# A rewritten order of VectorE's and GpSimd's work in the second attention slot of a fused graph-network kernel

## The reference

```
h = relu(layernorm(x))
# layer 0: each node takes the maximum over the features of its first 25 neighbours
idx, valid = top_k of (-column number) where adj != 0, 25 of them
agg = max over the valid neighbours of h ; max with 0 if the node has 25 neighbours or fewer
x = x + relu(concat[h, agg] @ W + b)
h = relu(layernorm(x))
# layer 1: attention of 8 heads of 16, open where adj, its transpose or the diagonal is set,
# then a feed-forward of 512 and two layernorms with scales and shifts
q, k, v = split(h @ Wqkv.T + bqkv)
attn = softmax(where(adj | adj.T | eye, q k / 4, -inf)) @ v
y = layernorm(h + attn @ Wo.T + bo) ; y = layernorm(y + relu(y @ W1.T + b1) @ W2.T + b2)
x = x + y
```

## Time and profile before

| what | value |
|---|---|
| median of 3 runs | 1257.94 us (1255.73 to 1259.4) |
| the profiled execution | 1255.8 us, span 1253.8 us |
| mean granted TensorE clock | 0.943 |
| TensorE matmul busy | 1043.9 us, 83% |
| VectorE busy | 797.5 us, 64% |
| ScalarE busy | 805.7 us, 64% |
| GpSimd busy | 737.4 us, 59% |

### The profile page before, as it was taken

How to read it: one execution, slowest core, us unless ns; L and a number is a source line. 1 busy time by engine, 2 the same in 40 slices (tenths; PEclk the granted TensorE clock), 3 DMA queues, 4 the chain that set the end, 5 groups by cost and what they waited for, 6 DMA issues and landing times.

```text
span 1253.8 us, 29308 instructions
## 1 busy us (share of the span) xinstructions
PE 1043.9 (83%) x11014; PEld 405.0 (32%) x11014; DVE 797.5 (64%) x3053; ACT 805.7 (64%) x1031; POOL 737.4 (59%) x741
## 2 busy tenths in 40 slices
PE   0125587688984989999999999999999999999874
PEld 0112331233331334343434333433343334333222
DVE  7856877767788477977797769776363534122323
ACT  1321257677852867788778877887678756875541
POOL 4776677567777777777777777776777520000000
PEclk9567889899996999999999999999999999999996
DMA  6533336426423433453345334431242110000000
GB/s 188 167 67 107 104 94 160 145 70 140 119 67 113 110 111 106 123 105 104 110 127 105 100 114 126 104 93 52 80 70 71 53 52 18 21 1 10 10 9 8
DMA packets 95156, 110.77 MB, mean 88 GB/s; under 512 B 17080, under 2 KB 75968, under 8 KB 94976
## 3 DMA queue, kind: packets, MB, share of 16 engines
q1 hardware_dynamic: 68352, 62.67, 16.4%
q0 software_dynamic: 22816, 44.61, 15.5%
q10 hardware_dynamic: 3808, 1.19, 0.4%
HBM read 91.10 MB, written 12.85 MB: 83 GB/s over the span
## 4 chain that ended last, share of the span: by engine, by line
PE 64%; ACT 11%; DVE 7%; POOL 7%; issue 6%; DMA 3%; SPq 0%; DVEq 0%; POOLq 0%; ACTq 0%
PE sc L1664 20%; PE cb L1684 13%; ACT probs L1460 10%; PE sc L1668 7%; PE m L1741 5%; PE m L1749 5%; POOL nb_low L716 3%; PE m L1570 3%; POOL nb_low L694 2%; PE m L1593 2%; DMA nb_low<-h_rows,lsorted 1%; PE m L1723 1%; PE m L1598 1%; PE m L1792 1%; PE m L1771 1%
## 5 line engine op out<-in xcount | busy, mean ns | idle before, releaser
L1460 ACT ACTIVATE probs<-sc 128x1024 f32<-128x1024 f32 x512 | 496.7, 1023 | 245.8 <-PE sc L1668 242.4
L694 POOL DMA_INDIRECT nb_low<-h_rows,lsorted x474 | 470.3, 992 | 168.8 <-issue 129.1
L1684 PE MATMUL cb<-probs,va 128*17 128x512 f32 x2048 | 270.6, 600 | 4.1 <-issue 3.2
L1664 PE MATMUL sc<-q_near,k_g 32*128 32x512 f32 x1024 | 147.8, 647 | 21.4 <-ACT probs L1460 17.2
L1664 PE MATMUL sc<-q_far,k_g 32*128 32x512 f32 x1024 | 149.6, 654 | 16.9 <-ACT probs L1460 15.8
L1015 DVE TENSOR_REDUCE agg<-nb_low 128x128 f32<-128x1024 f32 (+10 forms) x58 | 96.3, 1660 | 60.2 <-DMA nb_low<-h_rows,lsorted 34.4
L1668 PE MATMUL sc<-barred,negident 32*32 32x512 bf16 x4096 | 112.5, 386 | 1.8 <-issue 1.8
L829 DVE MAX8 cand<-keys 128x8 f16<-128x128 f16 x512 | 105.3, 278 | 2.2
L716 POOL DMA_INDIRECT nb_low<-h_rows,first_lists x80 | 80.5, 1006 | 41.9 <-issue 22.5
L1668 PEld LDWEIGHTS sc<-barred,negident 32*32 32x32 bf16 x4096 | 35.4, 88 | 200.8 <-issue 200.8
L1452 ACT ACTIVATE barred<-m 128x512 bf16<-128x512 f32 x128 | 72.9, 608 | 39.5 <-PE m L1598 39.5
(11 more groups left out here) (180 smaller groups left out, 1442.2 us busy)
## 6 DMA issues: line engine op xcount, KB each, us to landing
adj_t<-in_adj_dram SPq DMA_DIRECT2D x64, 512.0 KB
nb_low<-h_rows,lsorted POOLq DMA_INDIRECT x474
xh<-in_x_dram SPq DMA_DIRECT2D x8, 512.0 KB
h_rows<-xh SPq DMA_DIRECT2D x8, 512.0 KB
hl<-h_rows SPq DMA_DIRECT2D x8, 512.0 KB
x<-in_x_dram SPq DMA_DIRECT2D x16, 256.0 KB
out_dram<-h2T SPq DMA_DIRECT2D x16, 256.0 KB, 3.2
ag<-pooled_rows SPq DMA_DIRECT2D x7, 512.0 KB
```

The lines of the kernel that those rows point to most:

```text
L694: pool.indirect_dma_start(out=dst, out_offset=None, in_=h_rows[0:(f + 1) * (N + 1), :], in_offset=bass.IndirectOffsetOnAxis(ap=lsorted[:, ...
L1460: nc.scalar.activation(probs[:, i % 2, 2 * pair:2 * pair + 2, :], sc[:, 2 * pair:2 * pair + 2, :], ACT.Exp, scale=SCALE).then_inc(s_probs, 1)
L1664: nc.tensor.matmul(sc[:, a, :], k[part, :], q[part, :], start=True, stop=False)
L1684: last = nc.tensor.matmul(cb[a * SPAN:a * SPAN + VW, :], va[:, u % 2, a, kt, :], probs[:, i % 2, a, :], start=(kt == 0), stop=(kt == T - 1))
```

## The change

1. VectorE's slot 1: `second_slot` has a new order and its end is written out as `second_slot_end`. Ahead of the linear part of graph 2 now stand only `list_tile(4, 0)`, `list_tile(4, 1)` and `merge_pair(0)`; tiles 2, 3 and 4 of graph 4 and `merge_pair(2)` come behind it. `context(1, 2)` stands ahead of graph 3's first pooled tiles. `add_input(0, 1)` comes before `pool_tile(2, 6)`, `first_norm(4)` behind `context(1, 1)`.
2. In slot 2, `context(1, 3)` comes ahead of `pool_tile(3, 3)`.
3. GpSimd gathers tile 7 of graph 2 before it scatters graph 3's lists; `send(2, 6)` follows the scatter, then `load_lists(3)`, `send(2, 7)` and `beta2(1)`. The paces of graph 2's tiles 5 to 7 and of graph 3's tiles 0 to 2 are earlier by up to three steps.
4. SyncE: graph 1's `turn_values` goes ahead of adjacency tile (3, 5) in slot 0; in slot 1 the tiles (4, 4) and (4, 5) go behind the x1 halves, and `turn_values(2, 0)` ahead of tile (4, 7).
5. Graph 2's rank steps are 21 and 22 in place of 19 and 21; ScalarE normalizes graph 3's x at steps 24 and 25 of slot 0 in place of 22 and 23 (`H_AT_3`).

```diff
-PACE_2 = [(25, 3, 0, 31), (32, 3, 1, 35), (35, 3, 1, 38), (38, 3, 1, 41), (41, 3, 1, 43), (43, 3, 1, 45), (45, 3, 2, 47), (49, 3, 0, 50)]
-PACE_3 = [(19, 4, 0, 24), (24, 4, 0, 26), (27, 4, 0, 29), (29, 3, 0, 31), (32, 3, 0, 34), (35, 3, 1, 37), (38, 3, 0, 39), (43, 3, 2, 45)]
+PACE_2 = [(25, 3, 0, 31), (32, 3, 1, 35), (35, 3, 1, 38), (38, 3, 1, 41), (41, 3, 1, 43), (42, 3, 0, 44), (44, 3, 0, 46), (46, 3, 0, 48)]
+PACE_3 = [(18, 4, 0, 23), (23, 3, 0, 26), (26, 3, 0, 29), (29, 3, 0, 31), (32, 3, 0, 34), (35, 3, 1, 37), (38, 3, 0, 39), (43, 3, 2, 45)]
...
+H_AT_3 = {24: (0, 4), 25: (4, 8)}
...
-RANK_AT = {0: (-2, 3, 7, 8), 1: (0, 0, 2, 4), 2: (0, 19, 21, None), 3: (1, 11, 12, None)}
+RANK_AT = {0: (-2, 3, 7, 8), 1: (0, 0, 2, 4), 2: (0, 21, 22, None), 3: (1, 11, 12, None)}
...
-                    for t in range(2, 6):
+                    for t in range(2, 5):
                         load_list_tile(3, t)
                     turn_values(1, 0)
+                    load_list_tile(3, 5)
...
-                        for t in range(2, 5):
+                        for t in range(2, 4 if s == 1 else 5):
                             load_list_tile(l, t)
...
+                    if s == 1:
+                        load_list_tile(4, 4)
+                        load_list_tile(4, 5)
                     if live(l):
                         load_list_tile(l, 6)
                         store_h_rows(l)
+                    if s == 1:
+                        turn_values(f, 0)
+                    if live(l):
                         load_list_tile(l, 7)
-                    if live(g) and live(f):
+                    if live(g) and live(f) and s > 1:
                         turn_values(f, 0)
...
-                        if t == T - 2 and f >= AHEAD:
+                        if t == T - 2 and f > AHEAD:
...
+                    if f == AHEAD:
+                        scatter_lists(f + 1)
+                        send(f, T - 2)
...
                             load_lists(f + 1)
+                        if f > AHEAD:
+                            send(f, T - 2)
                         if f >= AHEAD:
-                            send(f, T - 2)
                             send(f, T - 1)
+                        if f == AHEAD:
+                            beta2(f - 1)
...
+                    context(1, 0)
                     pool_tile(2, 3)
-                    context(1, 0)
                     crowded_tiles(3)
                     make_lists(3)
                     pool_tile(2, 4)
                     list_ranks(3)
+                    add_input(0, 0)
+                    pool_tile(2, 5)
                     list_tile(4, 0)
-                    add_input(0, 0)
-                    first_norm(4)
                     finish(0, 0)
-                    pool_tile(2, 5)
-                    list_tile(4, 1)
-                    merge_pair(0)
                     wide_maxima(1, 1)
+                    add_input(0, 1)
                     pool_tile(2, 6)
-                    add_input(0, 1)
-                    list_tile(4, 2)
+                    pool_tile(2, 7)
                     finish(0, 1)
                     context(1, 1)
-                    pool_tile(2, 7)
+                    list_tile(4, 1)
+                    first_norm(4)
+                    merge_pair(0)
+
+                def second_slot_end():
+                    linear(2)
+                    list_tile(4, 2)
                     list_tile(4, 3)
+                    context(1, 2)
+                    largest(2, 0)
                     merge_pair(2)
+                    largest(2, 1)
+                    low_levels(3)
+                    largest(2, 2)
+                    pool_tile(3, 0)
+                    largest(2, 3)
+                    products(2)
+                    flag(2)
+                    list_tile(4, 4)
+                    pool_tile(3, 1)
+                    list_tile(4, 5)
+                    merge_pair(4)
+                    pool_tile(3, 2)
+                    list_tile(4, 6)
+                    list_tile(4, 7)
+                    merge_pair(6)
...
+                    if s == 2:
+                        context(p, 3)
                     if live(f):
                         pool_tile(f, 3)
-                    if live(p):
+                    if live(p) and s != 2:
                         context(p, 3)
```

More of the change, by code:

```diff
@@ L592, in _ @@
                         load_pooled(f)
-                    if live(l):
+                    if live(l) and s > 1:
                         load_list_tile(l, 5)
@@ L1352, in _ @@
                         second_slot()
+                        second_slot_end()
+                        continue
                     else:
@@ L1358, in _ @@
                         list_tile(l, 4)
-                    if live(r) and s > 1:
+                    if live(r):
                         low_levels(r)
@@ L1362, in _ @@
                         linear(f)
-                    if live(r) and s == 1:
-                        low_levels(r)
                     if live(r):
@@ L1534, in _ @@
                         if live(l) and l not in (0, 2):
-                            for t in range(*(H_AT if l > 4 else H_AT_1).get(n, (0, 0))):
+                            for t in range(*(H_AT if l > 4 else H_AT_3 if l == 3 else H_AT_1).get(n, (0, 0))):
                                 first_norm(l, t)
```

## The result

The changed kernel takes 1264.88 us (median, 1261.43 to 1268.42) against 1257.97 us for the kernel before on the same chip (1255.67 to 1261.97): ratio 1.005, 95% interval 1.0034 to 1.0066. It is slower by 6.9 us, where 1.7 were forecast. The profiled execution took 1268.42 us, span 1266.7. In the windows of the changed kernel (columns as in the earlier trace rows) slot 1 is 13.9 us shorter, slot 0 is 10.3 us and slot 2 14.9 us longer.

The account below looks back on a forecast made before the run. TensorE sets the pace from slot 2 on, and saturated GpSimd covers slot 0. Slot 1's 8.9 us are given back at slot 2's step 3: 0.8 later plus 0.9 for the clock, 1257.94 + 1.7 = 1259.6 us, range 1252.5 to 1263.5.

Parts of the forecast that it names:

- slot 0 costed at nothing: Slot 0: TensorE's gain of about 4 us is worth nothing, since saturated GpSimd's line starts with ranks that don't move.
- The wait in place of the one at step 19: Slot 0: TensorE's 7.0 us wait for find_crowded(2) at step 19 goes and one at step 22 replaces it.
- Step 17, hidden: Slot 1, step 17: about 4 us of TensorE's 9.2 us wait for add_input(0, 1) go, hidden by the wait for ag.
- The load of `ag`, 3.4 us earlier: Slot 1, step 20: send(2, 7), and with it the load of ag, comes 3.4 us earlier; bounds 0 and 5.9.
- The rival that the lists' load holds back `send(2, 7)`: Slot 1: load_lists(3) waits longer for the scatters, so ag is no earlier than now; 1263.0 us, chance 0.14.
- The page's price of 2.0 us plus bytes: Slot 1: rival that scatters land this fast, ag 2.5 us earlier still; 1257.1 us, chance 0.06.
- Step 28, 5.5 us: Slot 1, step 28: TensorE's wait for context(1, 2) goes, and 5.5 us with it.
- The flag at 445 and slot 2 at 449.6: End of slot 1: flag(2) ends at 445.0 and slot 2 starts at 449.6, 8.9 us earlier.
- The tail, 28.1 us: Slot 2: VectorE's work from the flag to find_crowded(4) takes 28.1 us, so it is ready at 473.1.
- GpSimd's tile (3, 3) "adds nothing": Slot 2: GpSimd's tile (3, 3) lands before VectorE's tail needs it, adding nothing to the 28.1 us.
- Slot 2 gives the gain back at step 3: Slot 2, step 3: TensorE waits some 9.5 us for find_crowded(4) and goes on 0.8 us later than now.
- the rival that the gain holds: Slot 2: TensorE's 8.9 us from slot 1 survive; 1249.0 us, chance 0.18.

Follow-up runs that it names:

- e1: The changed kernel with graph 2's rank steps put back to 19 and 21: 1.0005 of the kernel before (0.9991 to 1.0019).
- e2: The kernel before with only graph 2's rank steps moved, to 21 and 22 in place of 19 and 21: 1.0031 of the kernel before.
- e10: e1's kernel with list tiles moved into VectorE's idle times ahead of pool_tile(2, 5) and the linear part: 1.0005 of the kernel before.
- e15: e10 with the edits of e13 and e14, plus wide maxima, context(1, 3) and find_crowded(4) ahead of the last list tiles and merge: 0.9991 of the kernel before.
- e16: e15 with residual(1) also ahead of pool_tile(3, 4) in slot 2: 1.0002 of the kernel before (0.9983 to 1.0021).
- e9: Repetition of e1, the changed kernel with graph 2's rank steps back at 19 and 21, beside later kernels: 1.0017 of the kernel before.
- e14: e10 with find_crowded(4) ahead of pool_tile(3, 3) in slot 2: 0.9998 of the kernel before (0.9984 to 1.0012).
- e13: e10 with low_levels(3) ahead of context(1, 2) in VectorE's slot 1: 0.9999 of the kernel before (0.9985 to 1.0012).

## Why the prediction was wrong

**The step that failed** is the first: slot 0 costed at nothing, because GpSimd's "scatter of graph 2's lists starts with VectorE's ranks, which do not move". They moved by 6.1 us, counted from step 10, and the first gather by 5.3. The cover named there was the right one to look at, and GpSimd was as saturated as said; but its line starts with the ranks, and the ranks need TensorE twice (the transposition of `full`, the counts). Putting these two crossings two steps and one step later put the ranks later, and with them the whole line. The prediction had looked at VectorE's order alone, and met TensorE's steps "again at step 22" as if that were free. What e1 and e2 measured for this term is 4 to 5.7 us, where 0 stood; with it the forecast would have been 1263.6 to 1265.3, and 1264.9 was measured. That this fits so well is in part luck: the two errors below, 2 us too little for the load of `ag` and 3.3 us left out at step 17 of slot 2 (in the profiled execution), go against each other.

**The wait in place of the one at step 19** was forecast at step 22 for `full`. It came at step 20, for the bank that `context(0, 1)` holds; the bank's reader stands behind the very work that the new steps were to wait for no more.

**Step 17, hidden:** 2.7 us are left of 9.2 there, and the wait for `ag` is longer, 10.7. Right.

**The load of `ag`, 3.4 us earlier:** from GpSimd's first gather to the first use of `ag` it is 134.1 us before and 128.7 after, so 5.4 us, the upper end of what was allowed (5.9). Of the 2.0 us that the forecast was short of this, 1.1 are the landing of the scatters, 3.4 us in place of 4.5, and 0.8 the row of issues ahead of them, which took a little less than 1.3 us each. The rival that the lists' load holds back `send(2, 7)` fell: 1.05 us of idle time. The page's price of 2.0 us plus bytes ("DMA: Bandwidth & Descriptors" of the Trainium skill, the gpsimd path), by which the scatter would have landed before `send(2, 6)` is out (an estimate from the page), does not hold here either: the load starts 3.4 us behind the scatter's start, 1.05 us of it idle, which lies between that estimate and slot 0's 4.5.

**Step 28, 5.5 us:** the wait is gone. VectorE now waits 0.9 us for TensorE ahead of `context(1, 2)`, at 434.72, not the other way. Right.

**The flag at 445 and slot 2 at 449.6:** 451.07 and 455.7. The prediction called itself wrong if the flag came later than 449, and this sign did come. Less the 8.7 us by which graph 2's gathers start later, and plus the 2 us by which the load of `ag` was better than forecast, both are within 1 us of it.

**The tail, 28.1 us:** 28.4. Right. But the sentence that GpSimd's tile (3, 3) "adds nothing" was a tie: VectorE waited 0.29 us for it, and e10, whose tail was shorter, waited 2.7 us for it. With the tail cut the gather was next.

**Slot 2 gives the gain back at step 3:** the wait came, in three pieces of 3.7 us (for `context(1, 3)`), 2.7 (issue) and 2.2 (for `full`) in place of one of 9.5, and the rival that the gain holds fell. In e1, without the late ranks, TensorE is 11.1 us ahead at the start of slot 2 and 0.9 behind at step 5, much as forecast. The reason was too small, though. It is not only VectorE's moved work that takes the time back: e15 and e16 removed what held step 3 and still ended at 0.999 and 1.000. The prediction said "GpSimd is saturated" for the stretch to 370 and did not follow the line on to 494.

**"Everything behind it follows as before":** from step 5 to step 17 it does. Then the profiled execution loses 3.3 us at step 17, which e1 and e9 do not. The chain leads there from GpSimd's gathers between 517 and 523 us over VectorE's `turned`; why in this kernel and not in e1 stays open.

**Slots 3 to 7 as long as now:** right. Behind slot 2 the two kernels differ by under 1 us.

## What to carry to other kernels

When a request is moved to a later step to save the asker a wait, follow the answer: who on the other engine needs it, and which saturated line starts with that. Moving the request to be rid of a 7 us wait on TensorE cost 4 to 6 us here. If several reorderings each remove the wait they aim at and the time stays, look for the engine whose gaps are all issue, over the whole stretch and not only up to the next wait; count its instructions and gaps, and the most that another order can take out of its stretch is what is left (under 2 us of 224 here). Then ask whether it leads: compare the end with steps ahead of and behind it, since everything in the same stretch moves with the end.

## What the runs showed of the hardware that was not expected

**A copy of the keys took 4.07 us in place of 1.2**, beside an addition on GpSimd. VectorE's and GpSimd's timelines of the changed kernel, slot 2, and of the kernel before, slot 1:

```profile
513.93 4.07 DVE L839 SCALAR_TENSOR_TENSOR keys<-adj_t,prio 128x1024 f16<-128x1024 int32 x1
514.53 2.38 POOL L731 TENSOR_TENSOR x<-x,bias_rows 128x1024 f32<-128x1024 f32 x1
```
```profile
382.56 2.36 POOL L723 TENSOR_TENSOR x<-x,bias_rows 128x1024 f32<-128x1024 f32 x1
383.85 2.16 DVE L825 SCALAR_TENSOR_TENSOR keys<-adj_t,prio 128x1024 f16<-128x1024 int32 x1
```

The Trainium skill, "SBUF — State Buffer", on SBUF's two separate sides, says that VectorE and GpSimd share a pair of ports as an exclusive lock and that the one that starts first keeps it. The traces agree that they collide and that one waits for the whole of the other: in both cases VectorE's copy ends 1.09 us behind the end of GpSimd's addition, which keeps its usual length. The kernel before agrees with the order too, since the addition starts first there. The changed kernel does not show that order: VectorE's instruction is recorded 0.6 us earlier, and it is the one drawn out (0.6 + 2.38 + 1.09 = 4.07 us).

**TensorE at the lower clock after a wait**: the eight matmuls of a score pass take 2.09 us behind the 7.9 us wait of slot 0 (250.32 above), where the granted clock is 0.50 (1.2 GHz), and 1.14 us 5 us later, where it is 1.00 (2.4 GHz):

```profile
255.34 1.14 PE L1700 MATMUL sc<-q_far,k_g 32*128 32x512 f32 x8
```

**The same code differs between executions by up to 6 us.** Step 10 of slot 0 starts at 201.4 in e14, at 205.7 in e15 and at 207.2 in e16, which are alike up to there, at 201.5 in the kernel before and at 204.8 in the changed one, whose execution has a wait for a load of `va` in it:

```profile
PE cb L1720 <- DMA va<-v_rows: 2.2, 1, 2.2
```

And among e1, e9, e10 and e13 to e16, alike through slot 0, GpSimd's first gather lies 69.3 to 72.1 us behind that step. Between single profiles of this kernel a difference under 3 us means little, so each row above is read from a common point of its own trace, and which kernel is faster is told by the ratios alone.
